# Attention steps of one core: statistics a batch ahead, value products split around the scores, and a new order of TensorE's products

## The reference, cut to what matters

```
h = concat(patchify(x) @ W.T + b, txt)                 # (32, 113, 256)
a = layernorm(h)
q, k, v = rope(a @ Wq.T), rope(a @ Wk.T), a @ Wv.T      # 16 heads of 16
h = h + (softmax(q k^T / 4) v) @ Wo.T
l = layernorm(h) @ phi_w.T + phi_b                      # as (tokens, 64, 32)
h = h + softmax(l, over experts) @ experts(softmax(l, over slots)^T layernorm(h))
```

## Time and profile before

| what | us |
|---|---|
| median of three runs | 932.53 |
| the profiled execution, its own time | 930.55 |
| its span | 928.9 |
| start of the score products of step 0, 5, 31 | 35.67, 78.92, 290.60 |
| mean granted clock over the span | 0.988 |

### The profile page before, as it was taken

One profiled execution on the slowest core, in us unless ns is written; L12 is line 12 of the kernel. 1 busy time (PEld: TensorE's weight loads), 2 busy tenths in 40 slices (PEclk: granted clock), 3 DMA queues, 4 the chain that ended last, 5 costly groups with the idle time before them and its releaser, 6 DMA issues.

```text
span 928.9 us, 21774 instructions
## 1 busy us (share of the span) xinstructions
PE 902.2 (97%) x7684; PEld 744.1 (80%) x7684; DVE 719.7 (77%) x1085; ACT 493.1 (53%) x795; POOL 529.1 (57%) x512
## 2 busy tenths in 40 slices
PE   8989999999998989999999999999999999999997
PEld 7777887888886656888888888888888758888885
DVE  3577777777875788999999999999999865555552
ACT  1255555554554356666766667667676473333331
POOL 1375333233231277999999999999999671001000
PEclk9999999999998979999999999999999999999999
DMA  8611111111111235433232332323336997777760
GB/s 253 209 28 46 44 43 41 42 40 45 43 49 37 63 73 167 127 93 86 69 103 64 89 88 64 102 72 82 88 106 186 374 368 255 245 227 232 231 187 18
DMA packets 99925, 110.98 MB, mean 119 GB/s; under 512 B 12216, under 2 KB 91156, under 8 KB 93860
## 3 DMA queue, kind: packets, MB, share of 16 engines
q1 hardware_dynamic: 97760, 106.23, 37.3%
q0 software_dynamic: 1376, 3.70, 1.1%
q10 hardware_dynamic: 740, 0.41, 0.1%
HBM read 72.06 MB, written 38.21 MB: 119 GB/s over the span
## 4 chain that ended last, share of the span: by engine, by line
PE 90%; POOL 3%; DVE 2%; issue 2%; DMA 2%; ACT 1%; SPq 0%; DVEq 0%; ACTq 0%; POOLq 0%
PE slots_p_sum L1450 22%; PE slots_logits L1481 16%; PE slots_p_turn L1593 11%; PE slots_p_turn L1601 6%; PE attend_p_qk L568 5%; PE slots_p_turn L1435 5%; PE attend_p_row L568 4%; PE attend_p_score L549 3%; PE attend_p_score L540 3%; PE attend_p_k L560 3%; PE embed_acc L148 2%; PE attend_p_qk L577 2%; PE slots_logits L1562 2%; PE attend_p_k L555 1%; PE attend_p_q L555 1%
## 5 line engine op out<-in xcount | busy, mean ns | idle before, releaser
L1450 PE MATMUL slots_p_sum<-slots_x,slots_disp 128*128 128x256 f32 (+1 forms) x928 | 214.0, 386 | 4.4 <-POOL slots_disp L1188 4.4
L1450 PEld LDWEIGHTS slots_p_sum<-slots_x,slots_disp 128*128 128x128 f32 (+1 forms) x928 | 173.4, 192 | 35.4 <-issue 9.3
L1183 POOL TENSOR_TENSOR slots_comb<-slots_comb,slots_cmax 128x1024 f32<-128x1024 f32 x56 | 108.1, 1950 | 18.7 <-DVE slots_cmax L965 17.3
L1593 PE MATMUL slots_p_turn<-slots_y_parts,slots_hi 128*128 128x512 f32 (+1 forms) x464 | 111.0, 391 | 0.0
L446 POOL TENSOR_TENSOR attend_stack<-attend_rope_a,attend_rope_b 113x128 f32<-113x128 f32 x128 | 54.5, 459 | 86.5 <-DVE attend_rope_b L396 86.5
L1195 POOL TENSOR_TENSOR slots_comb<-slots_comb,slots_csum 128x2048 f32<-128x2048 f32 x27 | 97.8, 3621 | 5.9 <-DVE slots_csum L942 5.9
L1188 POOL TENSOR_TENSOR slots_disp<-slots_disp,slots_dsum 128x2048 f32<-128x2048 f32 x27 | 98.5, 3649 | 0.0
L1593 PEld LDWEIGHTS slots_p_turn<-slots_y_parts,slots_hi 128*128 128x128 f32 (+1 forms) x464 | 84.0, 186 | 18.0 <-DVE slots_lo L1114 0.4
L1234 POOL DMA_DIRECT2D out<-slots_o x29 | 15.9, 547 | 143.5 <-DVE slots_o L1100 143.5
L952 DVE TENSOR_TENSOR slots_disp<-slots_logits,slots_dmax 128x512 f32<-128x512 f32 x112 | 77.4, 691 | 4.6
L1481 PE MATMUL slots_logits<-phi_hi,slots_xt_hi 128*128 128x512 f32 x224 | 77.2, 426 | 1.9 <-ACT slots_comb L1303 1.9
(11 more groups left out here) (173 smaller groups left out, 1843.7 us busy)
## 6 DMA issues: line engine op xcount, KB each, us to landing
combine_t<-slots_ct SPq DMA_DIRECT2D x224, 128.0 KB, 2.4
slots_comb<-combine_t SPq DMA_DIRECT2D x14, 1024.0 KB, 5.6
slots_ct<-combine_t SPq DMA_DIRECT2D x14, 1024.0 KB, 5.7
slots_spare_w<-wexp SPq DMA_DIRECT2D x6, 1024.0 KB, 6.9
slots_disp<-wexp SPq DMA_DIRECT2D x6, 1024.0 KB, 8.6
expert_w<-wexp SPq DMA_DIRECT2D x4, 1024.0 KB, 11.1
h<-attend_h_out SPq DMA_DIRECT2D x32, 113.0 KB
slots_h_t<-h SPq DMA_DIRECT2D x28, 128.0 KB, 2.2
```

Source lines behind the costliest of these rows:

```text
L1183: nc.gpsimd.tensor_tensor(m, m, cmax[0:rows, shalf(i)].unsqueeze(2).broadcast_to([rows, SLOTS // 2, EXPERTS]), ALU.subtract).then_inc(csub ...
L1450: last = nc.tensor.matmul(p_sum[u % 2][:, i, :], disp[d][part].rearrange("p n s -> p (n s)")[:, 128 * block:128 * block + 128], x[d][part] ...
L1593: return nc.tensor.matmul(p_o[c % 2][0:rows], hi[c % 2][:, e, 0:rows], y_parts[:, e].rearrange("p i c -> p (i c)"), start=e == 0, stop=e = ...
```

## The change

It has four parts.

1. Statistics. `measure` is new on VectorE: it waits for a batch's load and computes the mean and variance. Step b measures batch b+4 (after normalising b+3, before the rotation; in steps up to 0 at the step's end), where before it measured b+3 right before normalising it. The first batch is measured ahead of all steps. VectorE's loop ends two steps earlier (`behind` 5), the rest being unrolled.
2. `finish` moves behind `qmax` in VectorE's order.
3. Value weighing is split: at the end of step b only the first two groups of heads of batch b are weighed, the other two after the scores of step b+1. In step 31 all four are weighed at the end.
4. TensorE's order: the value product goes ahead of the turn of the queries; the turn of the weighted values goes behind the turn of the keys; the query-key product runs in one piece behind the shifted scores.

TensorE's order in a step after the change: scores; weighing of two groups of batch b-1; value product; turn of the queries; output projection; turn of the maxima; turn of the keys; turn of the weighted values; shifted scores; query-key product; turn back; transpose of the normalised batch; weighing of two groups of batch b.

```diff
--- before.py
+++ after.py
@@ -259,7 +259,7 @@
         if not isinstance(n, int) or n > 0:
             eng.wait_ge(which, val(n))
 
-    def steps(eng, step, enter, follow, last=BATCH + 2):
+    def steps(eng, step, enter, follow, last=BATCH + 2, behind=3):
 
 
 
@@ -270,10 +270,10 @@
             if b <= 0:
                 enter(eng, b)
             straight(b)
-        with eng.Fori(0, (BATCH - 8) // 2) as k:
+        with eng.Fori(0, (BATCH - 5 - behind) // 2) as k:
             for c in (5, 6):
                 step(Count(k, 2, c), lambda n, c=c: Count(k, 1, (c + n) // 2), c % 2, [True] * 6)
-        for b in range(BATCH - 3, last):
+        for b in range(BATCH - behind, last):
             straight(b)
             follow(eng, b)
 
@@ -347,6 +347,13 @@
                 dve.wait_ge(h2_out[par], val(16 * half(-2)))
             nc.vector.tensor_tensor(h_out[par][:], wo_ps, h_res[par][:], ALU.add).then_inc(h2_ok, 1)
 
+        def measure(turn, par):
+
+            dve.wait_ge(h_ld[par], val(32 * (turn + 1)))
+            nc.vector.bn_stats(stats[:], h_in[par][:]).then_inc(stats_ok, 1)
+            dve.drain()
+            nc.vector.bn_aggr(mv[:], stats[:]).then_inc(mv_ok, 1)
+
         def low(b, normalises):
 
             dve.wait_ge(ont_hi_ok, val(b))
@@ -361,8 +368,6 @@
                 nc.vector.tensor_reduce(maxima[:, :, DH:DH + GROUPS],
                                         p_score[:, :, 0:GROUPS * T].rearrange("p j (g t) -> p j g t", t=T),
                                         AX_X, ALU.max, negate=True).then_inc(max_ok, 1)
-            if finishes:
-                finish(b)
             if scores:
 
                 dve.wait_ge(qmax_ps_ok, val(b + 1))
@@ -370,18 +375,19 @@
                 wait_for(dve, shifted_ok, b)
                 nc.vector.tensor_tensor(qmax[:], qt[par][:], p_q[:, 0, 0:T].unsqueeze(1).broadcast_to([128, GROUPS, T]),
                                         ALU.add).then_inc(qmax_ok, 1)
+            if finishes:
+                finish(b)
             if adds:
                 add(b, half, par, turns)
+            measured_next = not isinstance(b, int) or b + 4 < BATCH
             if normalises:
 
-                dve.wait_ge(h_ld[1 - par], val(32 * (half(3) + 1)))
-                nc.vector.bn_stats(stats[:], h_in[1 - par][:]).then_inc(stats_ok, 1)
-                dve.drain()
-                nc.vector.bn_aggr(mv[:], stats[:]).then_inc(mv_ok, 1)
                 dve.wait_ge(rstd_ok, val(b + 4))
                 wait_for(dve, xt_ps_ok, b + 2)
                 nc.vector.tensor_scalar(xn[1 - par][:], h_in[1 - par][:], mv[:, 0:1], rstd[:], ALU.subtract,
                                         ALU.mult).then_inc(xn_ok, 1)
+            if measured_next and (not isinstance(b, int) or b > 0):
+                measure(half(4), par)
             if isinstance(b, int) and b < 0:
                 e_vector(dve, b)
             if projects:
@@ -406,6 +412,8 @@
                 dve.wait_ge(xt_hi_ok, val(b + 4))
                 nc.vector.tensor_tensor(xt_lo[1 - par][:], xt_ps, xt_hi[1 - par][:].bitcast(F32),
                                         ALU.subtract).then_inc(xt_lo_ok, 1)
+            if isinstance(b, int) and b <= 0:
+                measure(half(4), par)
 
         dve.wait_ge(stack_clear, 3 + 2 * GROUPS)
 
@@ -413,7 +421,8 @@
             nc.vector.tensor_tensor(h_in[0][0:PATCHES, :], acc[0:PATCHES, 0:C], bias[0:PATCHES], ALU.add).then_inc(h_ld[0], 16)
 
         e_vector(dve, -4, first_rows)
-        steps(dve, step, lambda dve, b: b == 0 and e_vector(dve, b), follow, BATCH)
+        measure(0, 0)
+        steps(dve, step, lambda dve, b: b == 0 and e_vector(dve, b), follow, BATCH, 5)
         rest(lambda: finish(BATCH), lambda b: add(b + 2, lambda n: (b + 2 + n) // 2, b % 2, False), lambda: low(BATCH, False))
 
     def gpsimd(pool, follow):
@@ -598,15 +607,17 @@
                 wait_for(pe, exp_ok, 2 * b)
                 score(par)
             if finishes:
-                turn_values(b, turns)
+                for g in range(HALF, GROUPS):
+                    last = weigh_values(1 - par, g)
+                last.then_inc(pv_ok, 1)
             if turns:
+
+                pe.wait_ge(xt_lo_ok, val(b + 3) if projects else BATCH)
+                wait_for(pe, ont_lo_ok, b - 1)
+                split_product(v_ps, xt_hi[1 - par], xt_lo[1 - par], wv_hi, wv_lo).then_inc(v_ps_ok, 1)
                 pe.wait_ge(stack_ok, val(4 * (b + 2) - 2))
                 wait_for(pe, qmax_ok, b)
                 turn_stack(p_q, 1 - par, 0, q_ps_ok)
-
-                pe.wait_ge(xt_lo_ok, val(b + 3) if projects else BATCH)
-                wait_for(pe, ont_lo_ok, b - 1)
-                split_product(v_ps, xt_hi[1 - par], xt_lo[1 - par], wv_hi, wv_lo).then_inc(v_ps_ok, 1)
             if adds:
 
                 project_out(b)
@@ -618,6 +629,11 @@
                 pe.wait_ge(stack_ok, val(4 * (b + 2)))
                 wait_for(pe, ot_ok, b)
                 turn_stack(p_k, 1 - par, 1, k_ps_ok)
+            if finishes:
+                turn_values(b, turns)
+            if scores:
+                pe.wait_ge(qmax_ok, val(b + 1))
+                shifted_score(par)
             if projects:
 
                 pe.wait_ge(xt_lo_ok, val(b + 3))
@@ -625,12 +641,7 @@
                     pe.wait_ge(on_ok, val(b))
                 else:
                     wait_for(pe, rope_ok, b + 2)
-                split_product(p_qk[:], xt_hi[par], xt_lo[par], wqk_hi, wqk_lo, (0,))
-            if scores:
-                pe.wait_ge(qmax_ok, val(b + 1))
-                shifted_score(par)
-            if projects:
-                split_product(p_qk[:], xt_hi[par], xt_lo[par], wqk_hi, wqk_lo, (1, 2)).then_inc(qk_ok, 1)
+                split_product(p_qk[:], xt_hi[par], xt_lo[par], wqk_hi, wqk_lo).then_inc(qk_ok, 1)
             if finishes:
                 turn_back(b, turns)
             if isinstance(b, int) and b == BATCH - 1:
@@ -647,10 +658,12 @@
                 if turns:
                     pe.wait_ge(k_ok, val(b + 2))
                 pe.wait_ge(v_ok, val(b + 1))
-                for g in range(GROUPS):
+                final = isinstance(b, int) and b == BATCH - 1
+                for g in range(GROUPS if final else HALF):
                     pe.wait_ge(exp_ok, val(2 * b + g // HALF + 1))
                     last = weigh_values(par, g)
-                last.then_inc(pv_ok, 1)
+                if final:
+                    last.then_inc(pv_ok, 1)
 
         e_tensor(pe, -4)
         steps(pe, step, e_tensor, follow, BATCH)
```

## The result

The changed kernel takes 936.57 us (median of 5 runs, 935.38 to 937.57) against 932.25 for the kernel before on the same chip (5 runs, 928.66 to 932.60). The ratio is 1.0059, with a 95% interval of 1.0038 to 1.0079: slower by about 0.6%, where 935.5 and "slower" were forecast. The profiled execution took 936.82 and its span is 935.1, 6.2 longer than the 928.9 of before.

The account below looks back on a forecast made before the run. TensorE, busy 97%, was taken as the bound. Start +2.1, loop +1.0 and end 0 gave +3.1, 930.55 to 933.65 profiled; with 1.98 for the runs' median 935.6, forecast as 935.5 us, range 929.3 to 938.6.

Parts of the forecast that it names:

- The turn of the maxima: TensorE in a loop step: waits for ScalarE's query copy and starts 3.52 after the scores, a new wait of 0.16.
- The other step of each loop turn: Second step of each loop turn: has 0.20 of waiting where the first has 0.28, so loses a little more.
- The step that failed: TensorE's loop step: 8.11 to 8.16 against 8.09, taken as +0.04 a step over 24 steps, +1.0.
- Half weighing 0.57: TensorE's split weighing: each half takes 0.57, half of 0.95 being 0.48, plus 0.09 for a change between products.
- Rival C: Loop: VectorE becomes the bound, reduction late by 0.1 to 0.2 each step; +5.7, 938.2; chance 0.12.
- The wait for the deviation: Loop: the removed wait was off TensorE's path, so removing it is worth 0.
- The start, +2.1: First steps, to step 5's scores: measurement delays step 1's rotation 1.2, two cycles 1.36, half weighing returns 0.48.
- rival D: Clock at the end: less waiting could return up to 3.3, 932.3, or a slower stretch elsewhere lose it; chance 0.08.
- The end, 0: Steps 30 and 31: scores of 31 about 0.3 earlier, VectorE's chain late by the same; 0, bounds -0.4 and +0.4.
- A: Loop: no wait for the query copy, extra change free, step 7.85; -3.7 in all, 928.8; chance 0.15.
- B: Loop: copy wait hidden in part, steps of 8.02; +0.4 in all, 932.9, no change; chance 0.13.
- E: Start: the phi cycle absorbs the measurement, +1.0 only, 933.5, no change; chance 0.07.

Follow-up runs that it names:

- s8_third_ahead: The changed kernel with the queries' turn between the first third of the value product and the other two: 930.86 us, ratio 0.9998 to the kernel before.
- s6_best: The changed kernel with the edits of s8_third_ahead and s7_stats_off_path together: 925.92 us, ratio 0.9944 to the kernel before.
- s7_stats_off_path: The kernel before plus part 1, measuring ahead of the rotation in steps -1 and 0, behind it in steps 1 to 4: 931.89 us, ratio 1.0003.
- s2_no_stats: The changed kernel without part 1, statistics again measured right before the normalisation: 947.68 us, ratio 1.0183 to the kernel before.
- s1_stats_only: The kernel before with part 1 of the change alone, statistics measured a batch ahead: 934.99 us, ratio 1.0056 to the kernel before.
- s4_queries_first: The changed kernel with the turn of the queries ahead of the value product again: 933.96 us, ratio 1.0045 to the kernel before.
- s5_no_split: The changed kernel with all four groups of heads weighed at the end of the step: 936.07 us, ratio 1.0059 to the kernel before.
- s3_behind_rotation: The changed kernel with the measurement behind the rotation in steps 1 to 4: 934.52 us, ratio 1.0050 to the kernel before.
- the first four experiments: s1_stats_only, s2_no_stats, s3_behind_rotation and s4_queries_first, run on one chip and sharing 18 runs of the kernel before, median 929.15 us.

## Why the prediction came out right, point by point

The direction and both causes were right: a new wait for the query copy in the loop, and the measurement on the critical cycle at the start. The sum was too small, +3.1 where the two profiled executions differ by 6.3, and that the number came out near is in part luck.

- **The turn of the maxima, "with 0.06 to signal (my value; bounds 0 and 0.15) the maxima turn at 3.52: a new wait of 0.16".** The place and the releaser are right. The signal is 0.05 in one step of each loop turn (3.51) and 0.15 in the other (177.66 - 174.06 = 3.60).
- **"The other step of each loop turn ... loses a little more".** Right in sign, not in size: it loses 0.20 (8.24 to 8.44), the first 0.08 to 0.09 (8.09 to 8.17).
- **The step that failed: "Keys to 3.94, weighted values with one change to 4.56. ... So the step is 8.11 to 8.16 against 8.09. ... I take +0.04 a step".** The term is mis-sized: +0.143, just inside its bound of +0.15. After a wait the keys' turn comes 0.19 to 0.25 behind the maxima's, not 0.10: the records show the weight load at the product's own start and the semaphore instruction behind it, where without a wait both are ahead. So the shifted scores start at 4.70 (187.20 - 182.50) and 4.78 instead of 4.56. Two smaller terms nearly cancel in this: the keys' turn takes 0.41 and not 0.32, the turn of the weighted values 0.53 and not 0.62. s8_third_ahead, where the maxima's turn doesn't wait, has 0.10 there and 0.257 less in the step. The forecast priced the wait by its length and left out what TensorE's queue had done under cover of the work before it.
- **"`on` ... so that the query-key product needn't wait".** Nearly: `on` ends at 188.11 (VectorE's at 187.69 takes 0.42 like the one at 179.23), the shifted scores hold the queue to 188.19, the product starts at 188.25, 0.06 late; in the other step it isn't late.
- **Unbroken query-key product, "less what a run unbroken saves, at most 0.06".** A third takes 0.46 to 0.55 and the three 1.45 to 1.48, where the prediction had 1.47 to 1.53. It is right, and with the 0.28 of waiting gone it is what s8_third_ahead and s6_best cash in.
- **Half weighing 0.57.** 0.53 and 0.52; whole, it takes 0.92. The idea is right; the price was 0.13 for both, against the 0.19 that 0.57 twice implies.
- **VectorE: "the next reduction can start about 9.2, just when the scores ... are there".** It starts 1.13 after the scores (183.63) and ends 0.3 before the maxima's turn. Rival C fails: VectorE is not the bound. (The "cover of 0.02 above" that C names stands nowhere in the prediction.)
- **"The wait for the deviation ... worth 0".** Right for the kernel before (s7_stats_off_path), wrong as a statement on the change: there, without part 1 it is worth 0.58 a step (s2_no_stats). The prediction weighed each part against the kernel before, and not against the kernel that the other parts make.
- **The measurement in the loop, free.** Right (s1_stats_only).
- **The start, +2.1: "1.2 + 1.36 - 0.48".** Term by term, in s4_queries_first: the rotation of step 1 comes 1.45 later against the scores of step 0, not 1.2; the two cycles add 1.30, not 1.36; the half weighing gives back 0.39, not 0.48. That makes 2.36, and its start is +2.39. With TensorE's old order (s1_stats_only) the rotation of step 1 comes only 0.87 later; why the new order adds to that isn't taken apart further. s1_stats_only has no half weighing, 0.87 + 1.30 = 2.17, so that its +2.17 is near +2.1 is chance; s5_no_split has none either, and its start is +2.68.
- **The clock at the start, which only rival D allowed for.** The change's own profiled execution has +3.5, 1.15 more: it ran steps 0 and 1 in 18.34 where s3_behind_rotation and s4_queries_first, with the same order there but for the queries' turn and the place of step 1's measurement, took 17.19, and it alone of the three has 3.5 of half clock in them. So the score products of step 5 stand at 82.61, not near 81.0.
- **The end, 0.** The last three steps cost +0.2, and the rest of the span gave 1.0 back. In step 30 TensorE's wait for the exponentials isn't less but in two pieces, 0.56 ahead of the half weighing and 0.22 ahead of the scores of 31, where it was 0.79 in one (answering to the earlier trace rows). The slower clock isn't gone but longer: 10.3 at 0.50 from 298.20, instead of 6.8 from 295.70.

```profile
297.01 0.60 PE L569 MATMUL attend_p_k<-attend_prob_t,attend_vp 113*32 113x113 f32 x16 [0.56 <-ACT attend_prob_t L489]
297.82 1.53 PE L549 MATMUL attend_p_score<-attend_kt,attend_qt 16*113 16x113 f32 x32 [0.22 <-ACT attend_prob_t L489]
```

- **The sum, +3.1 on the profiled execution.** 6.3 there (930.55 to 936.82), but 4.3 between the medians (interval 3.5 to 7.4). The loop term is 2.3 too small, and the clock at the start isn't in the sum. The prediction added 1.98 to go from the profile to the median of three runs; in later runs of the kernel before its median is 929.15 and 931.08, so that addition is as large as the scatter of such medians. 935.5 lies 1.1 from 936.57 in part by luck: profile against profile the sum is short by 3.2.
- **Rivals.** A (no waits, a step of 7.85) and B are out for the change, but half of A's mechanism is real: without the copy's wait the step is 8.05; its other half, that the extra change costs nothing, is not (0.13). E is out: the cycle of phi grew by all of the measurement. D's 3.3 didn't come back, as the slower stretch at the end is longer; of its other branch, a slower stretch elsewhere, there are the 1.15 at the start. The 1.0 that the rest of the span gave back is not the clock's by these rows: behind the last score products the change has 23.9 of half clock and the kernel before 20.5.

Open: why the clock fell at 42.2 in the change and at 39.6 in s8_third_ahead, and not in s1_stats_only, s3_behind_rotation, s4_queries_first and s5_no_split, which have the measurement ahead of the first reduction too. With one profile of each it can be chance. Also open: what made the rest of the span 1.0 shorter.

## What to carry to other kernels

When a piece is moved to fill a wait, follow the consumers of the piece that it pushes back: here the value product pushed the query turn by 0.8, and the copy of that turn was what the next user of its bank waited for; a third of the product in its place filled the same hole and left the copy in time. Price a new wait on a full engine by more than its length, since what the queue did under cover behind it (weight loads, semaphore instructions) comes into the open. A part that is worth nothing alone can be what the others need, and one whose cost lies in a start-up phase can be placed differently there for nothing.

## What the runs showed of the hardware

- TensorE's waiting product starts 0.05 or 0.15 after the end of ScalarE's copy, alternating with the two steps of the loop (steps 10 to 19 of the change), and 0.06 or 0.13 after the end of VectorE's reduction (the same steps of s5_no_split). The product behind the waiting one starts 0.19 to 0.27 after it, where it is 0.10 in most steps without a wait.
- The run times of the kernel before go with the mean granted clock: of the 18 runs beside the first four experiments the 9 at 0.989 or 0.990 lie at 927.55 to 929.28, the 5 at 0.983 or 0.984 at 931.94 to 932.40, the other 4 at 928.93 to 930.99. So its median depends on how many of the runs had the lower clock, and differences of 0.3% need a common chip and many runs.
- The rest of the span behind the last score products is 636.6 to 639.1 over the ten kernels, though the change and the experiments alter nothing in it but the order of step 31: 636.7 with 13.6 of half clock (s6_best), 639.1 with 26.1 (s7_stats_off_path). The half clock isn't all of it, as s5_no_split and the kernel before both have 20.5 and take 636.8 and 638.3.
